# A two-layer graph network on one core: x turned once, its own term added on VectorE, the layer norm folded behind the u product, the neighbour sum by column chunks, and x and w1 requested at once

## What is computed

```
agg = segment_sum(x[src], dst)                      # 1250 x 512
h0  = (1 + eps) * x + agg
h1  = relu(batch_norm(h0 @ W1 + b1, g1, be1))       # 512 -> 1024, norm over the nodes
h2  = relu(batch_norm(h1 @ W2 + b2, g2, be2))       # 1024 -> 512
x1  = layer_norm(x + (x + h2))                      # over the 512 features
u   = relu(x1 @ LW1 + lb1)                          # 512 -> 256
h   = u @ LW2 + lb2                                 # 256 -> 512
out = layer_norm(x1 + h + segment_sum(h[src], dst))
```

## Time and profile before

| | |
|---|---|
| median of 3 runs | 285.03 us (284.92 to 285.14) |
| the profiled execution | 287.6 us, of which the span from the first to the last instruction is 285.8 us |
| TensorE busy | 259.5 us, 1581 products |
| VectorE, ScalarE, GpSimd busy | 144.4, 123.0, 76.6 us |
| mean granted clock of TensorE | 0.985 |

### The profile page before, as it was taken

The page is one execution under the profiler, slowest core; times in us unless marked ns, Lnnn a source line. Parts: engine busy times, 40 slices in busy tenths (PEclk is TensorE's granted clock), DMA queues, the critical chain, the costliest instruction groups (busy, mean ns, idle before and its releaser), DMA issues.

```text
span 285.8 us, 4044 instructions
## 1 busy us (share of the span) xinstructions
PE 259.5 (91%) x1581; PEld 221.6 (78%) x1581; DVE 144.4 (51%) x348; ACT 123.0 (43%) x217; POOL 76.6 (27%) x73
## 2 busy tenths in 40 slices
PE   0657999998999999999999999999769999999991
PEld 0636998886888888888888888888649888888770
DVE  1588997552743144444443313004474545448884
ACT  1407353424867047555556220200445445342694
POOL 5420000000920006565656700048301211112120
PEclk9999999999999999999999999999986999999998
DMA  4276000000056810000003795009000000000044
GB/s 139 93 277 240 0 2 0 2 0 6 2 203 236 274 42 1 2 0 0 2 20 126 254 234 102 0 19 202 11 1 2 1 0 2 0 0 2 3 180 175
DMA packets 21846, 20.43 MB, mean 71 GB/s; under 512 B 13911, under 2 KB 14846, under 8 KB 21826
## 3 DMA queue, kind: packets, MB, share of 16 engines
q1 hardware_dynamic: 21320, 19.91, 22.8%
q0 software_dynamic: 160, 0.13, 0.2%
q10 hardware_dynamic: 346, 0.10, 0.2%
HBM read 10.94 MB, written 5.92 MB: 59 GB/s over the span
## 4 chain that ended last, share of the span: by engine, by line
PE 81%; DVE 7%; ACT 5%; DMA 4%; issue 1%; DVEq 0%; SPq 0%; POOLq 0%
PE ps L1006 19%; PE ps L993 19%; PE ps L941 17%; PE ps L1078 7%; PE ps L1067 6%; PE ps L893 3%; PE ps L923 2%; PE ps L1052 2%; DVE hot_s L683 2%; PE ps L1125 2%; DMA src_i<-in_src 2%; PE ps L1043 1%; DMA pairs<-pair 1%; DMA run<-pairs,start_i 1%; PE ps L1064 1%
## 5 line engine op out<-in xcount | busy, mean ns | idle before, releaser
L758 DVE BATCH_NORM_STATS2 stats<-ps 128x6 f32<-128x500 f32 (+1 forms) x36 | 21.6, 599 | 63.1 <-PE ps L1006 35.2
L941 PE MATMUL ps<-AT,xh 128*128 128x500 f32 (+1 forms) x120 | 45.2, 385 | 0.0
L941 PE MATMUL ps<-AT,xl 128*128 128x500 f32 (+1 forms) x120 | 42.8, 364 | 0.0
L993 PE MATMUL ps<-h0h,wh 128*128 128x500 f32 (+1 forms) x96 | 34.0, 354 | 0.0
L993 PE MATMUL ps<-h0h,wl 128*128 128x500 f32 (+1 forms) x96 | 33.8, 352 | 0.0
L993 PE MATMUL ps<-h0l,wh 128*128 128x500 f32 (+1 forms) x96 | 33.7, 351 | 0.0
L443 ACT ACTIVATE AT<-ps 128x500 fp32r<-128x500 f32 x25 | 14.8, 590 | 32.3 <-PE ps L923 32.3
L941 PEld LDWEIGHTS ps<-AT,xl 128*128 128x128 f32 x120 | 24.3, 202 | 2.5
L941 PEld LDWEIGHTS ps<-AT,xh 128*128 128x128 f32 x120 | 24.2, 202 | 2.5
L1006 PE MATMUL ps<-a1h,wl 128*128 128x500 f32 (+1 forms) x96 | 24.9, 354 | 0.0
L1006 PE MATMUL ps<-a1l,wh 128*128 128x500 f32 (+1 forms) x96 | 24.8, 354 | 0.0
(11 more groups left out here) (141 smaller groups left out, 528.8 us busy)
## 6 DMA issues: line engine op xcount, KB each, us to landing
turns<-half_out SPq DMA_DIRECT2D x10, 320.0 KB, 2.2
xs<-in_x SPq DMA_DIRECT2D x1, 2304.0 KB
out<-xs SPq DMA_DIRECT2D x9, 256.0 KB
w1s<-in_L_gnn_W SPq DMA_DIRECT2D x1, 2048.0 KB, 10.4
w2s<-in_L_gnn_W SPq DMA_DIRECT2D x1, 2048.0 KB, 8.3
xs<-in_x SPq DMA_DIRECT2D x1, 1280.0 KB, 7.9
xs<-in_x SPq DMA_DIRECT2D x1, 1024.0 KB
lws<-in_L_gnn_W SPq DMA_DIRECT2D x1, 512.0 KB, 3.6
```

What stands on the lines that cost most here:

```text
L758: link(nc.vector.bn_stats(stats[:, 6 * c:6 * c + 6], ps[:, zbank(t, c), 0:c1 - c0]))
L941: last = mm(o, part[0:r, k, d * P:d * P + P], AT[0:r, k, c0:c1], start=False, stop=(k == NT - 1 and j == 1), skip_group_check=True)
L993: last = mm(ps[:, zbank(t, c), 0:c1 - c0], w[:, t, d * P:d * P + P], h[c][:, d, :], start=(d == 0 and j == 0), stop=(d == DT - 1 and j == 2))
```

## The change

- **x turned once.** TensorE transposes x tile by tile (`x_cols`, 40 transposes: 20 before the windows' runs are awaited, 20 between build 1 and build 2), ScalarE copies it to `xT` (`x_turn`). `xT` stays in memory; x isn't read a second time, and h2 isn't turned to rows by itself.
- **Own term.** `own` and `diag` go. VectorE adds (1 + eps) xT to the item in PSUM (`h0_own`), behind `h0_sum` and ahead of the high part. In the slots it comes one slot after the item, the high part two, the low part three. In the tail it stands in VectorE's order behind the diagonal adds and ahead of the low part.
- **Requests.** SP requests both halves of x, w1 and both biases in a row, with no wait for GpSimd. w2 comes in pieces of one tile, four in flight; lw1 and lw2 at other places.
- **Second layer** unsplit: `z_part` and the last order go. The last batch norm takes all three chunks after the last product.
- **Norm folded.** 2 xT + h2 stays transposed (`xp_sum`) and is split as it is (`xph`, `xpl`). lw1 is centred over its input features: a sum on VectorE (`lw1_sum`), a product with a matrix of 1/512 on TensorE, and a subtraction (`lw1_center`). Then u = relu(r (xp @ centred lw1) + lb1) with each row's r = 1/std, applied when u is evicted (`u_scale`, VectorE). `hidden_early` makes the first three quarters of that product for all tiles directly behind the second layer, `hidden_last` the rest. Rows are still turned, for the statistics and for x1 (`xp_rows`, two banks in turn, a tile's bank free when ScalarE has written x1), but u doesn't pass through them. `keep_warm` goes.
- **Neighbour sum by chunks** of 512, 512 and 226 columns: the first chunk tile by tile while rows are made, the others behind it, with the products of LW2 of finished chunks in between.
- GpSimd takes ReLU of u and its low part (two instructions a tile), and LW2's low part after them.

The core of the diff:

```
-            sp.wait_ge(lb1_zero, 1)
-            for row in (0, 32):
-                sp.dma_start(lb1r[row:row + 1, :], lb1.rearrange("(o d) -> o d", o=1)).then_inc(lb1_in, 16)
-            sp.wait_ge(runs_asked, 1)
             sp.dma_start(xs[:, half:NT - 1, :], x[half * P:full, :].rearrange("(t p) d -> p t d", p=P)
                         ).then_inc(x_in2, 16)
             sp.dma_start(xs[0:rows[-1], NT - 1, :], x[full:N, :]).then_inc(x_in2, 16)
             sp.dma_start(w1s[:, :, :], w1.rearrange("(k p) n -> p k n", p=P)).then_inc(w1_in, 16)
+            sp.dma_start(lb1_all[:, :], lb1.rearrange("(o d) -> o d", o=1).broadcast_to([P, L])).then_inc(lb1_in, 16)
...
+            def x_turn(k):
+                r = rows[k]
+                act.wait_ge(x_turned, k + 1)
+                nc.scalar.activation(xT[:, :, P * k:P * k + r],
+                                     ps[:, x_bank(k), :].rearrange("p (d c) -> p d c", c=P)[:, :, 0:r],
+                                     ACT.Copy).then_inc(xT_set, 1)
...
                     group_out(g)
                     if half + g < NT:
                         x_high(half + g)
-                    for i in items_after[g]:
+                        x_turn(half + g)
+                    for i in h0_after(g - HIGH_LAG):
                         h0_high(i)
...
+            def h0_own(i):
+                c, d = divmod(i, DT)
+                c0, c1 = CH[c]
+                v.wait_ge(h0_sum, i + 1)
+                if i == 0:
+                    v.wait_ge(xT_set, NT)
+                o = ps[:, 2 + i % RING, 0:c1 - c0]
+                nc.vector.scalar_tensor_tensor(out=o, in0=xT[:, d, c0:c1], scalar=eps1[:, 0:1], in1=o,
+                                               op0=ALU.mult, op1=ALU.add).then_inc(h0_own_set, 1)
...
             for j in range(DT):
                 for k in range(j * each, min(NT, (j + 1) * each)):
                     loops(k)
+                h0_own(NI - DT + j)
                 h0_low(NI - DT + j)
...
+            for d in range(DT):
+                batch_norm(HT + d)
+                xp_sum(d)
+                if d == 0:
+                    lw1_sum()
+                if d == 1:
+                    lw1_center()
+                if d == 2:
+                    lw1_low()
+            v.wait_ge(xph_set, DT)
+            nc.vector.tensor_tensor(xpl[:, DT - 1, :], xT[:, DT - 1, :], xph[:, DT - 1, :].bitcast(F32),
+                                    ALU.subtract).then_inc(xpl_last, 1)
...
+            for s in range(NT + 2):
                 if s < NT:
                     ln_stats(s)
+                if s >= 2:
+                    u_scale(s - 2)
+                if s < NT:
+                    ln_scale(s)
...
             for g in range(2):
                 build(g)
+            for k in range(half, NT):
+                x_cols(k)
             pe.wait_ge(flag_set, 1)
-            own(0, 0, half)
...
+            for k in range(5):
+                hidden_early(k)
+            for k, row in ((5, 0), (6, 1), (7, None), (8, 2), (9, None)):
+                hidden_early(k)
+                if row is not None:
+                    xp_rows(row)
+            for j in range(NT // 2):
+                hidden_last(j)
+                for k in (2 * j + 3, 2 * j + 4):
+                    if k < NT:
+                        xp_rows(k)
+                if j >= 1:
+                    neighbours(0, 2 * j - 2)
+                    neighbours(0, 2 * j - 1)
+            for k in (NT - 2, NT - 1):
+                neighbours(0, k)
+
+            for k in range(half):
+                neighbours(1, k)
+            for k in range(2):
+                second(k)
+            for k in range(half, NT):
+                neighbours(1, k)
+            for k in range(2, 6):
+                second(k)
+            for k in range(NT):
+                neighbours(2, k)
+            for k in range(6, NT):
+                second(k)
```

More of the change, by code:

```diff
@@ L594, in ln2_root @@
+            sq = [u32[:, 2 * i:2 * i + 2, :].rearrange("p a b -> p (a b)") for i in range(2)]
             def ln2_root(k):
@@ L822, in _ @@
-            v.wait_ge(x_again, 32)
-            for s in range(NT + 1):
+                v.wait_ge(u_sum, k // 2 + 1)
+                if k == 0:
+                    v.wait_ge(lb1_in, 16)
+                if k >= UR:
+                    v.wait_ge(ul_set, k - UR + 1)
+                nc.vector.scalar_tensor_tensor(out=u32[0:r, k % UR, :], in0=u_at(k), scalar=ln_r[0:r, k, 0:1],
+                                               in1=lb1_all[0:r, :], op0=ALU.mult, op1=ALU.add).then_inc(u32_set, 1)
+            for s in range(NT + 2):
@@ L913, in _ @@
             last.then_inc(counted, 1)
-            own(DT, 0, half)
             def build(g):
@@ L954, in _ @@
                         build(g)
-                    if g >= 2 and DT + g - 1 < RING:
-                        own(DT + g - 1, 0, half)
                     for u in slot_units[g]:
@@ L976, in _ @@
                 pe.wait_ge(AT_set, NG)
-                for i in range(RING):
-                    own(i, 0, half)
                 for u in units[0:(len(CH) - 1) * per]:
@@ new lines, in hidden_early, with hidden_last, xp_rows @@
+            def hidden_early(k):
+                if 2 * (k // 2) == 4:
+                    pe.wait_ge(act_set, 2 * BT - 2)
+                for d in range(DT - 1):
+                    hidden(k, d)
+            def hidden_last(j):
+                if j == 0:
+                    pe.wait_ge(xph_set, DT)
+                    pe.wait_ge(xpl_last, 1)
+                for k in (2 * j, 2 * j + 1):
+                    last = hidden(k, DT - 1)
+                last.then_inc(u_sum, 1)
+            def xp_rows(k):
```

562 lines of the change are left out of this document (267 added, 295 removed).

## The result

The changed kernel takes **295.24 us** (median of 4 runs, 293.66 to 297.91), against 285.08 for the kernel before beside it: ratio 1.033, 95% interval 1.028 to 1.039. The forecast was 282.6 with a range of 278.5 to 287.5. The result is slower by 10.2 us and outside the range.

A forecast was written before the change was run, and what follows sets the result against it. TensorE, 81% of the chain that ended last, was taken as the bound. 285.8 + 1.5 - 0.8 + 0.45 - 3.6 = 283.4 us of span; -2.45 carried to the median of 285.03 gave 282.6 us, range 278.5 to 287.5.

The forecast's parts named there:

- x and w1 at once: Start: 3.5 MB more queued over the pair store and gather; +1.5 us, for the first gather, bounds 0 and 8.7.
- rival (b): Start: pair store and gather each wait behind much of the 3.5 MB; 5 us, total 286.1; chance 0.20.
- Aggregation 1.3 later: Before aggregation: x's early transposes and their PSUM copies start it 1.3 us later, bounds 0 and 2.9.
- The tail: Aggregation's last chunk: TensorE idles about 2.8 us for the last low part, so of 7.4 us 0.8 arrive: -0.8 us.
- rival (c): After the stall at 94 us: clock falls, 7 us at the low level cost 3.4 more, total 286; chance 0.13.
- The mean product: Before the last second-layer product ends: one float32 product of 256 columns for the mean, +0.45 us.
- The end: From the last second-layer product's end (Z) to the kernel's end: 79 us against 82.6, so -3.6 us.
- To row 2: From the last second-layer product's end to the third row's transposes: 13.8 us at the high clock.
- Rows 2 to 9: From the third row's transposes to the tenth row's: 19.7 us at the high clock.
- The ring: Row stage: each row costs the loop left by two PSUM banks, 2.8 us, replacing 5.1 us of TensorE.
- Last u: From the tenth row's transposes to the end of u's last low part: 6.8 us.
- Rest: From the end of u's last low part to the end of the span: 35.7 us.

The follow-up runs named there:

- Experiment 3: Changed kernel with VectorE taking the own term ahead of the same turn's diagonal adds in the aggregation's tail; 291.12 us.
- best kernel: Changed kernel with bulk requests after the gathers, own term before diagonals, neighbour chunks one per row, VectorE's affine before its scaling, bias rows behind v's first low part; 277.80 us.
- experiment 4: Changed kernel with one neighbour chunk behind each row's transposes instead of two chunks behind two rows; 292.33 us.
- experiment 11: Changed kernel with 18 TensorE products that nobody reads added around the third to fifth rows; 294.06 us.
- experiment 10: The best kernel with 18 TensorE products that nobody reads added around the third to fifth rows; 277.66 us.
- experiment 12: Changed kernel with the bias rows behind VectorE's first low part of v instead of ahead of it; 290.37 us.
- experiment 8: Changed kernel with bulk requests after the gathers, own term first, chunks spread, VectorE's affine first, and waits holding GpSimd's casts and the bias rows; 280.49 us.
- gathers alone: Changed kernel with SP requesting x's second half and the weights only after GpSimd has issued the second gather; 293.16 us.

## Why the prediction failed, step by step

**x and w1 at once: forecast +1.5, measured +4.3 to +4.9.** This is rival (b), which had a chance of 0.20 and a price of 5. The bounds, 0 to 8.7, held; the choice between them was wrong. I took the surcharge of one crowded store, whose last quarter ran on emptier engines, and gave the gather none. Measured, the store lost 3.5 us and the gather 1.9 against the kernel before (1.1 came back in gaps between the steps). The step that failed is the reading that the old store ran beside full engines for three of its four us, and so had shown what a crowd costs. In the kernel before the bulk thins out during the store (rows of 1 us, columns as above):

```profile
8.00:9.00 1.00, 1.00 (x5) 0.97 (x5) 0.63 (x4) 0.00 (x0) 0.00 (x0) 1.00 0.63 226
9.00:10.00 1.00, 0.13 (x1) 0.00 (x0) 0.93 (x6) 0.55 (x2) 0.00 (x0) 1.00 0.08 21
```

The old store, asked at 5.95, landed at 9.87 us, some 1.3 us after the bulk had ended; with the bulk going on it landed at 13.35. Nor were the engines idle for the 2.2 us that it was set against: the ten stores of the earlier trace rows were asked from 80.6 to 91.6 us, where the DMA share was 0.5 to 1.0 from 82 us on. The Trainium skill, "DMA: Bandwidth & Descriptors", section Queues, rings and completion order, has the engines serve the queues in turn by packets; I read from it a term near the lower bound. The trace agrees for the store, which lands 5 us before the bulk ends at about 18.3 us, but not that the turns are cheap; the gather lands at 19.36 us, behind that end, and doesn't show whether it waited for it.

**Aggregation 1.3 later: measured +0.5.** Right in kind, a little too dear. The twenty transposes took 3.87 us, where 4.3 were forecast, and 9.8 us from one-hot to aggregation was seen in the run with spread chunks, at the high clock.

**The tail: forecast -0.8, measured -0.2 at the third chunk (+4.1, of which +4.3 is the start's), and +1.9 behind it.** The mechanism was right to the instruction: ScalarE waits 1.01, 1.01 and 0.98 us for the own term. The size was off: TensorE's idle time was 4.54 us in place of 2.8. With the later start taken out, TensorE reached this place 1.2 us sooner than forecast (97.02 - 4.28 = 92.7 us for 93.9) and the last low part came 0.5 us later (101.5 - 4.3 = 97.2 for 96.7). Nor was the first item served at once: VectorE's two diagonal adds took 4.53 us from 80.83 beside GpSimd's subtraction, and the own term (L724) could start only at 85.28. The clock then fell to 0.52 for some 3 us, which is rival (c): from the third chunk to Z it is 108.0 us, 105.7 before, with 0.43 of it the mean product. Experiment 3 priced the fall at 1.5 us, not 3.4. That this part's gain was there to be had, 7.4 us less of TensorE's work, experiments 3 and 9 show: in the best kernel the third chunk starts at 91.2 us, 6.3 earlier than before.

**The mean product: +0.45.** Measured 0.43.

**The end: forecast Z+79, measured Z+86.5.** The four legs, forecast at the high clock against measured:
- *To row 2*, 13.8 against 14.8. The last sum into x and xpl took 2.12 and 2.17 us beside GpSimd's casts, where the sum has 1.46 for each: 1.4 us of a cause that the forecast didn't have (0.4 of it made good elsewhere).
- *Rows 2 to 9*, 19.7 against 25.2, or 22.7 if all 3 us that the forecast added for the low clock fall here: 2.5 us or more of miss. The ring was right: 2.66 us a row where nothing interferes (forecast 2.8), and 3.1 at the low clock. What failed is the sentence that the ring replaces TensorE's time: TensorE's own order was not laid out. Two neighbour chunks, eight products, stand as a block between the rows two by two, and at the low clock a block holds the next row for 3.3 us. The forecast has those blocks (3.5 in place of 1.9) but adds only their surplus. Spreading them took 4.1 us off this leg (experiment 4), holding the clock up 2.5 (experiment 11), and both together reach 18.6 (experiment 10), 4.1 below experiment 11 at the same clock.
- *Last u*, 6.8 against 10.6, the largest miss of one leg. GpSimd works off three rows one behind the other (8.2), which the forecast took as one, and its one slow subtraction (3.17) adds 2.4.
- *Rest*, 35.7 against 35.9: right.

So 7.5 us of miss behind Z, 2.8 at the start, and 2.4 between: the sum of 283.4 becomes 296.1. **The sign** hung on the end: -3.6 was the only large gain in the sum, and it rested on a ring of three engines drawn as if they met only at its hand-offs. The range fell short too: it reached over one rival at a time, and here (b), a part of (c) and the end went the same way together.

**A wait that was missed: VectorE and GpSimd on SBUF tiles at once.** The traces have it in three places: xpl's surplus behind a cast that had begun 0.37 us earlier, the cast's 2.21 us when the order was reversed (experiment 12), and the subtraction that started 0.17 us behind VectorE's first bias row and ended at 256.90, 0.61 us behind the fourth. Left without such company they take 1.46, 1.23 and 0.73 us. So the last-u leg lacked 2.4 us in the sum, and to row 2 lacked 1.4. The Trainium skill, "SBUF — State Buffer", section SBUF: two separate sides, describes a pair of SBUF ports that VectorE and GpSimd share as an exclusive lock, held for the whole instruction, with the later of the two fully blocked; for a VectorE instruction with two SBUF inputs this holds against a GpSimd instruction that reads SBUF. I did not weigh it. The trace agrees in the three places above.

What stays open: rows 2 to 9 of after vary by 1 to 2.6 us between runs whose edits don't touch them (24.0, 22.6, 23.9). The wait ahead of row 2 and the clock go together in all of these runs, but no run sets that wait by itself, and why 22.6 lies below the other two is not shown. Nor is shown what makes the clock at 24 to 40 us low in one execution and high in another.

## What to carry to other kernels

A small transfer on which everything hangs should have the DMA engines to itself; asking for bulk data "early since it is free" cost 4.3 to 4.9 us here, and a one-line wait got it back. When work moves from a full engine to three idle ones, write down each engine's order at the place where they meet: who stands ahead of whom in one program decided 5.3 us in the tail and 4.1 in the row stage, with the same instructions. And VectorE and GpSimd are better given their large SBUF tiles at different times, here by order rather than by waits; the waits of experiment 8 gave with one hand and took with the other.

## What the runs showed of the hardware

- An 83 KB store took 3.8 to 3.9 us where the bulk reads beside it ended 1.1 to 1.3 us before its landing (before, gathers alone), and 7.0 to 7.5 us where they went on, at 283 to 426 GB/s in stretches of 1 us. A gather took 3.3 to 3.9 us with next to nothing else on the DMA engines and 5.4 to 6.2 where the bulk was still going on when it started. It was so in both kernels.
- Sums, subtractions and casts of VectorE and GpSimd on SBUF tiles held each other off until the first had ended, whichever it was: from 1.46 to 2.17 us, from 1.23 to 2.21, from 0.73 to 3.17. A run of four VectorE instructions with gaps of nearly nothing held GpSimd off through all four.
- TensorE's granted clock fell to 0.52 behind an idle stretch of 4.54 us, and stayed at 1.00 behind one of 1.56. In the kernel before it stayed up behind 1.24 us, and with the wait taken away it was at 0.50 behind 1.97. Among the rows it was 0.61 in a stretch in which TensorE was busy for 10.0 of 15 us, and 1.00 with 18 products that nobody reads.
- The 17.4 us between the changed kernel and the best one are won with order and one added wait: no arithmetic differs between them.
